# Gathering routed expert rows later in a group, and loading the next heads last: one change to an attention and mixture-of-experts kernel

## The chip, the cores and the metric

The kernel runs on one core of a Trainium2 chip. The metric is the device time of one execution in microseconds (us). The times shown are three runs, with their median, and one more execution that the hardware profiler took.

## The reference

The input x is (2, 2048, 256) in float32. What is computed is

```python
xn = layernorm(x)                                   # over the last axis
q, k, v = split(xn @ Wqkv); q, k = rope(q), rope(k) # 16 heads of 16
attn = softmax(causal(q @ k.T * scale)) @ v         # 2048 x 2048 scores per head
gates = softmax(xn @ gate_w.T + gate_b)             # 10 gates, 8 of them with an expert
w, sel = top_k(gates, 2); w = w on the 8 experts, scaled to sum to 1
ffn = sum over the two selected: w * (xn @ expert_w[sel] + expert_b[sel])
out = x + (attn @ Wout + bout) + ffn
```

## The kernel before, in words

Three stages follow each other: `project` (layer norm, q, k, v, gates, routing), `attend`, and `output` (the last projection and sums). The change lies in `attend`, which also carries the experts.

**Groups and units.** `attend` walks through 8 groups `g` of 4 heads (`GROUPS`). A group has `NU` = 40 units; unit `u` is one block of 128 keys against a chunk `c` of 512 queries. The chunks are walked in the order `WALK = (3, 2, 0, 1)`, so the units of chunk 3 are 0 to 15, of chunk 2 16 to 27, of chunk 0 28 to 31, of chunk 1 32 to 39; `ends` = (15, 27, 31, 39). Units that touch the causal diagonal (`diag[u]` is not None) are 1, 5, 8, 12, 17, 19, 22, 25, 28 to 31, 33, 34, 36 and 38.

**One unit on the engines.** TensorE (PE) computes 4 score matmuls (`scores`, line 1465), ScalarE (ACT) exponentiates each into `probs` (line 1216), GpSimd (POOL) zeroes the part above the diagonal if the unit is a diagonal one (`mask`, line 1110), and PE multiplies with the values, 4 matmuls, which the trace has as 8 (`pv`, line 1520; "PV u" below). `probs` has 4 buffers. PE waits in `pv` of a diagonal unit for `masked`, a count that `mask` raises. Between them PE computes scores for row maxima ("q" items, lines 1425 and 1428) that VectorE (DVE) reduces (line 1271), through two slots of `psP`. The order of PE's work in a group is written out by hand, a letter each (`PE_ORDER`): s a score matmul, p a PV, digits the q items, m a turned maximum, o a chunk's output, x and y the turn of an expert's input and the expert itself. The kinds of the groups are plain, route, four times experts, plain, last. "route" is "plain" with two more items r, the first ahead of PV 0 and the second behind PV 11; so group 6 has the same order as group 1 from PV 0 to PV 10.

**The experts.** In groups 2 to 5 each group runs 9 (`EG`) pairs of expert tiles. The result of a pair is copied by ACT from PSUM into `yt` (line 1237), and SP stores it to `expert_scratch` in HBM (`store_e`, line 1053, semaphore `y_stored`), then loads the weights of the pair after next (`load_e`, lines 1047 and 1049, semaphore `e_in`). `yt`, the weights and the inputs all lie in the space of `xn`.

**SP's queue.** SP issues its DMAs in the order of `PE_ORDER`. Behind the last unit of chunk 2 and of the last chunk (`FREED`), it waits for `pv_ok` of that unit and calls `load(g + 2, ...)`: 12 DMAs for `Qs`, 12 for `Ks`, one for `Vs` (line 74 and line 1030). In the experts order, the last PV (39) stands ahead of the last y (pair 8), so the loads are issued ahead of that pair's store. `store_m` (line 1041) stores the row maxima of a chunk.

**The gathers.** Each token takes two rows of `expert_scratch`, the first into `xn` (i = 0), the second into space of `Qs`, `Ks`, `Vs` and `rest` (i = 1): 32 tiles of 128 tokens each, so 64 indirect DMAs on POOL's queue (`gather`, line 1120). `fetched` says behind which unit a gather stands: in group 6 tile t with i = 0, in group 7 tile t with i = 1, each at `SPOTS[t]`, one gather behind a unit. `SPOTS` is 0 to 27 and 32 to 37. `passed` waits for the unit's last exponential. Since the first gather overwrites `xn`, POOL waits at the head of group 6 (lines 1159 to 1163) until every expert result is stored and every expert load has landed. POOL's instructions run in order, so that wait stands ahead of group 6's first mask, that of unit 1.

The first rows of all tiles are used in group 7 (`add_first`), the second in `output`.

Of the kernel before, what the change touches and what calls it, by code (L numbers as in the profile page):

```python
# [34 lines left out]
TT = N // P  # L35
TILES = B * TT
# [5 lines left out]
GROUPS = B * HEADS // HG  # L42
# [15 lines left out]
ONE = 1  # L58
# [726 lines left out]
def attend(nc, qk_s, v_s, we_s, be_s, xd, ys, wout, escale, idx, unscale, etab, Qs, Ks, Vs, xn, acc, hot, ge, eye, later, identf,  # L785
           identh, wo, on, wsel, bo, second, lane, number, at):
    with ExitStack() as ctx:
# [61 lines left out]
        pv_ok = sem("pv_ok")  # L849
# [15 lines left out]
        e_in = pair("e_in")  # L865
        hi_ok = sem("hi_ok")
        y_stored = pair("y_stored")
# [7 lines left out]
        WALK = (3, 2, 0, 1)  # L875
        FREED = {2: 1, 1: 0}
# [5 lines left out]
        units = [(c, kt) for c in WALK for kt in tiles(c)]  # L882
        NU = len(units)
        diag = [kt - CT * c if kt >= CT * c else None for c, kt in units]
        q0s = [0 if d is None else d * P for d in diag]
        ends = [u for u in range(NU) if u == NU - 1 or units[u + 1][0] != units[u][0]]
# [100 lines left out]
        def is_item(order, at):  # L987
            x = order[at]
            return x[0] in "moxyr" or x[0] == "q" and any(y[:-1] == x[:-1] for y in order[:at])
# [28 lines left out]
        def _(sp):  # L1018
# [51 lines left out]
            for g in range(GROUPS):  # L1070
                j, r = divmod(g, 2)
                order = orders[KIND[g]]
                n = 0
                for at, x in enumerate(order):
                    if x[0] == "m":
                        store_m(slot_of(n), uses(g, n), M_TURN[x[1:]], r ^ x[1], x[2])
                    elif x[0] == "y":

                        buf, _ = pair_of(g, x[1])
                        sp.wait_ge(item_ok[slot_of(n)], ONE + uses(g, n) + 1)  # L1080
                        sp.sem_inc(carrier, 1)
                        store_e(buf, EG * (g - 2) + x[1])
                        if EG * (g - 2) + x[1] + 2 < MTILES_USED // 2:
                            load_e(buf, EG * (g - 2) + x[1] + 2)
                    elif x[0] == "pv" and x[1] in ends and units[x[1]][0] in FREED and g < GROUPS - 2:

                        u = x[1]
                        sp.wait_ge(pv_ok, PV0 + NU * g + u + 1)
                        sp.sem_inc(carrier, 1)
                        load(g + 2, r, FREED[units[u][0]])  # L1090
                        if g == 1 and u == ends[1]:

                            sp.wait_ge(ids_ok, ONE + 1)
                            sp.wait_ge(bt_ok, ONE + 2)
                            for i in range(2):
                                load_e(i, i)
                    n += is_item(order, at)
            sp.wait_ge(wo_in, ONE + 16)

        @block.gpsimd  # L1100
        def _(pool):
# [17 lines left out]
            def gather(t, i):  # L1119
                nc.gpsimd.indirect_dma_start(out=xn[:, t, :] if i == 0 else second(t), out_offset=None, in_=ys[:, :],  # L1120
                                             in_offset=bass.IndirectOffsetOnAxis(ap=idx[:, i, t:t + 1], axis=0)
                                             ).then_inc(y_in[i], 16)
# [26 lines left out]
                    fetch(n + 2)  # L1149

            turned = {}
            fetched = {(6 + i, SPOTS[t]): (t, i) for i in range(2) for t in range(TILES)}

            for n in range(TILES):
                tables(n)
            for g in range(GROUPS):
                if g == 2:
                    split(0)
                if g == 6:

                    for i in range(2):
                        pool.wait_ge(y_stored[i], ONE + 16 * EG * 2)
                        pool.wait_ge(e_in[i], ONE + 16 * LOADS_E * EG * 2)
                if g == 7:

                    pool.wait_ge(pv_ok, PV0 + NU * g)
# [1 line left out]
                for at_x, x in enumerate([("s", 0, i) for i in range(SB)] + order):  # L1168
                    if x[0] == "s" and x[2] == HG - 1 and x[1] < NU:
# [15 lines left out]
                                fetch(n)  # L1185
                        if (g, u) in fetched:
                            passed(g, u)
                            gather(*fetched[g, u])
                    elif x[0] == "x":
                        n = EG * (g - 2) + x[1]  # L1190
                        turned[n] = slot_of(m), uses(g, m)
# [543 lines left out]
```

## Time and profile before

| | |
|---|---|
| median of 3 runs | 1041.32 us (1041.28 to 1044.14) |
| the profiled execution | 1037.85 us |
| its span | 1036.1 us |
| PE busy | 920.9 us, 89% of the span |
| DVE busy | 861.9 us, 83% |
| ACT busy | 714.8 us, 69% |
| POOL busy | 457.9 us, 44% |

A row of a timeline begins with the start and the duration in us, then the engine, the line, the operation, what is written and read, and how many instructions are merged ("x8"). In brackets stands how long the engine was idle just before, and what released it ("issue": nothing that the profile shows). "PEld" is PE loading weights. In a row of windows, each engine's busy time stands for the stretch with the number of instructions, then PE's granted clock as a share of 2.4 GHz, then what the DMA engines did.

### The profile page before, as it was taken

To read this page: it belongs to the slowest core of one execution; us is meant where nothing else is said; L and a number is where in the kernel's file an instruction comes from. 1 tells how busy PE (TensorE), PEld (TensorE's weight loads), DVE (VectorE), ACT (ScalarE), POOL (GpSimd) and SP (SyncE) were. 2 spreads that over 40 slices of the span, in tenths; PEclk is the share of its full clock that TensorE was granted. 3 is DMA by queue.
4 is the path that set the end of the run, shared out by engine and by line. 5 is a ranking of instruction groups with operands and counts; after the bars stand their busy time and mean duration, and the time that the engine had idled before them with its cause. 6 is when DMAs were issued, how large, how long until landed. Compare 5 with 4: busy or idle time off the path is not lost. (4 is left out here: it accounts for less than half of the span.)

```text
span 1036.1 us, 22141 instructions
## 1 busy us (share of the span) xinstructions
PE 920.9 (89%) x7874; PEld 388.0 (37%) x7874; DVE 861.9 (83%) x1132; ACT 714.8 (69%) x1542; POOL 457.9 (44%) x588
## 2 busy tenths in 40 slices
PE   3888435999999999999999999999999799999988
PEld 1554311333433234344333433344434323333257
DVE  6999779899899887987788787878798599995776
ACT  3556200788788777886787677877788588889942
POOL 4677559555201244244724564263423145345510
PEclk9999755899999999999999999999999899999999
DMA  9767530300200334054313443164505221112113
GB/s 323 265 240 267 168 127 5 110 2 28 76 2 2 114 104 134 3 172 135 123 43 112 134 133 95 53 164 130 128 12 150 78 65 59 32 47 63 47 51 123
DMA packets 82277, 106.65 MB, mean 103 GB/s; under 512 B 10192, under 2 KB 59256, under 8 KB 81144
## 3 DMA queue, kind: packets, MB, share of 16 engines
q1 hardware_dynamic: 75640, 87.40, 26.6%
q0 software_dynamic: 6528, 17.83, 6.5%
q8 instruction: 64, 1.05, 0.4%
q14 instruction: 45, 0.37, 0.1%
HBM read 67.37 MB, written 37.50 MB: 101 GB/s over the span
## 5 line engine op out<-in xcount | busy, mean ns | idle before, releaser
L1271 DVE TENSOR_REDUCE blk<-psP 128x2 f32<-128x1024 f32 (+2 forms) x576 | 640.2, 1161 | 102.8 <-PE psP L1428 43.5
L1216 ACT ACTIVATE probs<-psS 128x512 f32<-128x512 f32 (+3 forms) x1280 | 588.2, 539 | 189.9 <-PE psS L1465 170.5
L1465 PE MATMUL psS<-Qs,Ks 50*128 50x512 f16 (+3 forms) x1280 | 322.5, 354 | 12.4 <-ACT probs L1216 9.4
L1425 PE MATMUL psP<-Ks,Qs 48*128 48x512 f16 (+3 forms) x1280 | 284.7, 365 | 39.0 <-DVE blk L1271 21.9
L1520 PE MATMUL psO<-probs,Vs 128*32 128x512 f32 (+3 forms) x2560 | 301.4, 546 | 5.9 <-POOL probs L1110 4.9
L1110 POOL TENSOR_SCALAR_AFFINE_SELECT probs<-probs 128x512 f32<-128x512 f32 x128 | 82.4, 644 | 355.0 <-ACT probs L1216 338.5
L1465 PEld LDWEIGHTS psS<-Qs,Ks 50*128 50x128 f16 x1280 | 92.9, 94 | 239.1 <-ACT probs L1216 145.2
L1425 PEld LDWEIGHTS psP<-Ks,Qs 48*128 48x128 f16 x1280 | 75.5, 95 | 155.2 <-DVE blk L1271 100.8
L1428 PE MATMUL psP<-later,eye 64*128 64x128 bf16 x1024 | 91.0, 223 | 0.0
L1520 PEld LDWEIGHTS psO<-probs,Vs 128*32 128x32 f32 x2560 | 51.8, 108 | 87.1 <-issue 67.6
L1133 POOL DMA_INDIRECT xn<-norm_scratch,ids x72 | 69.5, 966 | 20.7 <-issue 11.5
L1428 PEld LDWEIGHTS psP<-later,eye 64*128 64x128 bf16 x1024 | 72.1, 99 | 16.9 <-issue 2.4
L1125 POOL TENSOR_SCALAR xn<-lane,at 128x128 f16<-128x128 f32 x64 | 38.6, 604 | 47.7 <-issue 24.1
L1497 PE MATMUL psP<-xn 128*128 128x256 f16 x432 | 57.3, 273 | 0.9 <-DVE xn L1306 0.9
L720 PE MATMUL psQ<-xp,wqp 128*128 128x512 f16 x192 | 47.6, 394 | 10.5 <-DVE turn L562 5.9
L1120 POOL DMA_INDIRECT xn<-expert_scratch,idx x32 | 30.4, 949 | 39.7 <-ACT probs L1216 20.9
L1497 PEld LDWEIGHTS psP<-xn 128*128 128x128 f16 x432 | 39.3, 98 | 21.4 <-DVE blk L1271 10.4
L1146 POOL TENSOR_TENSOR xn<-xn 128x512 f16<-128x512 f32 x36 | 41.8, 1161 | 3.0
L562 DVE TENSOR_TENSOR turn<-psQ,trig 128x1024 f32<-128x1024 f32 x32 | 38.4, 1218 | 2.6 <-DVE part L567 1.8
L1128 POOL TENSOR_SCALAR xn<-lane,at,number 128x76 f16<-128x76 f32 x64 | 39.5, 617 | 0.0
L1237 ACT COPY xn<-psP 128x512 f32<-128x512 f32 x36 | 21.1, 586 | 26.5 <-PE psP L1499 25.6
L364 POOL TENSOR_TENSOR turn<-turn 128x512 f32<-128x512 f32 x16 | 24.0, 1502 | 23.0 <-DVE turn L562 22.7
(171 smaller groups left out, 742.0 us busy)
## 6 DMA issues: line engine op xcount, KB each, us to landing
xn<-we_scratch SPq DMA_DIRECT2D x72, 256.0 KB
expert_scratch<-xn SPq DMA_DIRECT2D x36, 256.0 KB
v_scratch<-vst SPq DMA_DIRECT2D x8, 1024.0 KB, 4.0
qk_scratch<-part SPq DMA_DIRECT2D x32, 256.0 KB, 4.0
Vs<-v_scratch SPq DMA_DIRECT2D x16, 512.0 KB, 3.9
Ks<-qk_scratch SPq DMA_DIRECT2D x192, 32.0 KB
Qs<-qk_scratch SPq DMA_DIRECT2D x192, 32.0 KB
acc<-x SPq DMA_DIRECT2D x8, 512.0 KB, 9.1
```

The lines of the kernel that those rows point to most:

```text
L720: ins = pe.matmul(out, lhs(x, w, k), rhs(x, w, k), start=(n == 0), stop=(n == len(todo) - 1))
L1110: nc.gpsimd.affine_select(out=v, in_=v, compare_op=ALU.is_ge, fill=0.0, base=0, pattern=[[0, HG], [1, P]], channel_multiplier=-1).then_inc ...
L1128: nc.gpsimd.tensor_scalar(at_tile[:, n, :], lane[:, 0:MTILES], at[:, 0, n:n + 1], number[:, t:t + 1], ALU.is_equal, ALU.mult).then_inc(lis ...
L1133: nc.gpsimd.indirect_dma_start(out=xt[n % 2][:, t, :], out_offset=None, in_=xd[:, :], in_offset=bass.IndirectOffsetOnAxis(ap=ids[:, 2 * n ...
L1146: nc.gpsimd.tensor_tensor(xs[n % 2][:, 1, :], rows, xs[n % 2][:, 0, :], ALU.subtract).then_inc(x_split, 1)
L1216: nc.scalar.activation(probs[u % NPR][:, h, q0:CH], psS[:, n % SB, q0:CH], ACT.Exp, scale=exp_scale).then_inc(s_read[n % SB], 1)
L1271: nc.vector.tensor_reduce(out, src, AX.X, ALU.max).then_inc(item_ok[slot], 1)
L1425: ins = pe.matmul(psP[:, slot, at:at + w], Qs[r][rows, qt // CT, p, t * P:(t + 1) * P], Ks[r][rows, kc, p, 0:w], start=True, stop=True)
L1428: ins = pe.matmul(psP[:, slot, at + w - P:at + w], eye[all_rows, i, :], later[all_rows, i, :], start=False, stop=True, skip_group_check=True)
L1465: pe.matmul(psS[:, n % SB, q0:CH], Ks[r][rows, kt // CT, p, kt % CT * P:(kt % CT + 1) * P], Qs[r][rows, c, p, q0:CH], start=True, stop=Tru ...
L1497: pe.matmul(psP[:, slot, t * D:(t + 1) * D], xT[buf][:, w0, at_k:at_k + P], wt[2 * buf + t][:, of:of + D], start=(n == 0), stop=False)
L1520: ins = pe.matmul(psO[h * VW:(h + 1) * VW, q0:CH], Vs[r][:, kt, h * VW:(h + 1) * VW], probs[u % NPR][:, h, q0:CH], start=(kt == 0), stop=e ...
```

## The change

Two things are moved. On SP, the load for group g + 2 that follows the last unit of a group is issued at the very end of the group, behind all stores and expert loads. On POOL, the wait for the expert results moves from the head of group 6 to unit 6, and the 32 first-row gathers, which stood one behind each of 32 units from unit 0 on, stand two behind each of the 16 units 6 to 21. Group 7's gathers stay as they were.

```diff
-                    elif x[0] == "pv" and x[1] in ends and units[x[1]][0] in FREED and g < GROUPS - 2:
+                    elif x[0] == "pv" and x[1] in ends[:-1] and units[x[1]][0] in FREED and g < GROUPS - 2:
...
+                if g < GROUPS - 2:
+
+                    sp.wait_ge(pv_ok, PV0 + NU * g + NU)
+                    load(g + 2, r, FREED[WALK[-1]])
...
-            fetched = {(6 + i, SPOTS[t]): (t, i) for i in range(2) for t in range(TILES)}
+
+            fetched = {(6, SPOTS[6 + t]): [(2 * t, 0), (2 * t + 1, 0)] for t in range(TT)}
+            fetched.update({(7, SPOTS[t]): [(t, 1)] for t in range(TILES)})
...
-                if g == 6:
-
-                    for i in range(2):
-                        pool.wait_ge(y_stored[i], ONE + 16 * EG * 2)
-                        pool.wait_ge(e_in[i], ONE + 16 * LOADS_E * EG * 2)
...
                         if (g, u) in fetched:
                             passed(g, u)
-                            gather(*fetched[g, u])
+                            if (g, u) == (6, SPOTS[6]):
+
+                                for i in range(2):
+                                    pool.wait_ge(y_stored[i], ONE + 16 * EG * 2)
+                                    pool.wait_ge(e_in[i], ONE + 16 * LOADS_E * EG * 2)
+                            for t, i in fetched[g, u]:
+                                gather(t, i)
```

## Rows read from the trace of the kernel before

**Rows 1.** Waits of PE, 205 to 1010 us: total us, times, longest.
```profile
PE psO L1520 <- POOL probs L1110: 4.9, 3, 4.4
```
**Rows 2.** Timeline of PE where group 6 begins: PV 0 and PV 1.
```profile
815.71 1.06 PE L1520 MATMUL psO<-probs,Vs 128*32 128x512 f32 x8
...
825.60 1.93 PE L1520 MATMUL psO<-probs,Vs 128*32 128x512 f32 x8 [4.42 <-POOL probs L1110]
```
**Rows 3.** Timeline of POOL, same stretch: the first work of group 6.
```profile
823.91 0.98 POOL L1120 DMA_INDIRECT xn<-expert_scratch,idx  x1 [16.69 <-issue]
824.89 0.66 POOL L1110 TENSOR_SCALAR_AFFINE_SELECT probs<-probs 128x512 f32<-128x512 f32 x1
825.71 0.94 POOL L1120 DMA_INDIRECT xn<-expert_scratch,idx  x1 [0.16 <-issue]
826.96 0.95 POOL L1120 DMA_INDIRECT xn<-expert_scratch,idx  x1 [0.30 <-issue]
```
**Rows 4.** Timelines of ACT and SP, same stretch.
```profile
811.80 0.59 ACT L1237 COPY xn<-psP 128x512 f32<-128x512 f32 x1 [1.02 <-PE psP L1499]
...
810.25 4.07 SPq L74 DMA_DIRECT2D Qs<-qk_scratch  x12
...
818.97 0.51 SPq L1053 DMA_DIRECT2D expert_scratch<-xn  x1
```
**Rows 5.** Windows: PV 0 to 1, 1 to 3, 3 to 10, in groups 1 and 6.
```profile
278.31:283.71 5.40, 5.09 (x45) 2.15 (x45) 4.01 (x6) 3.91 (x9) 0.55 (x1) 1.00 0.42 124
283.71:288.66 4.95, 4.67 (x35) 1.11 (x34) 4.81 (x5) 4.16 (x10) 0.09 (x1) 1.00 0.19 55
288.66:304.28 15.62, 15.20 (x140) 4.52 (x140) 15.19 (x18) 13.30 (x30) 1.84 (x3) 1.00 0.01 2
815.71:825.60 9.89, 5.16 (x46) 2.14 (x45) 6.02 (x7) 5.94 (x12) 1.63 (x2) 0.79 0.40 116
825.60:832.83 7.23, 7.20 (x34) 1.42 (x34) 3.21 (x3) 3.10 (x8) 3.89 (x5) 0.58 0.31 90
832.83:848.45 15.62, 15.20 (x140) 4.51 (x140) 15.23 (x17) 13.27 (x30) 8.44 (x10) 1.00 0.21 60
```
**Rows 6.** Timeline of POOL in group 6: gathers of units 6, 7 and 24, mask of unit 25.
```profile
835.11 0.95 POOL L1120 DMA_INDIRECT xn<-expert_scratch,idx  x1 [0.65 <-ACT probs L1216]
837.57 0.95 POOL L1120 DMA_INDIRECT xn<-expert_scratch,idx  x1 [1.51 <-ACT probs L1216]
...
875.87 0.95 POOL L1120 DMA_INDIRECT xn<-expert_scratch,idx  x1 [1.37 <-ACT probs L1216]
876.99 0.64 POOL L1110 TENSOR_SCALAR_AFFINE_SELECT probs<-probs 128x512 f32<-128x512 f32 x1 [0.17 <-issue]
```
**Rows 7.** Timeline of PE in group 6: PV 17, 19 and 22.
```profile
862.37 1.06 PE L1520 MATMUL psO<-probs,Vs 128*32 128x512 f32 x8
867.63 0.85 PE L1520 MATMUL psO<-probs,Vs 128*32 128x384 f32 x8
874.68 0.64 PE L1520 MATMUL psO<-probs,Vs 128*32 128x256 f32 x8
```
**Rows 8.** Timeline of DVE around PV 17 to 22 of group 6.
```profile
867.50 8.61 DVE L1271 TENSOR_REDUCE blk<-psP 128x2 f32<-128x768 f32 x8 [0.47 <-PE psP L1428]
```
**Rows 9.** Timeline of SP and PE, end of group 4 into group 5: first load, last weight load, third expert.
```profile
701.56 4.09 SPq L74 DMA_DIRECT2D Qs<-qk_scratch  x12
...
703.52 0.59 ACT L1237 COPY xn<-psP 128x512 f32<-128x512 f32 x1 [1.43 <-PE psP L1499]
...
720.70 0.29 SPq L1049 DMA_DIRECT2D xn<-be_scratch  x1
...
733.39 0.83 PE L1497 MATMUL psP<-xn 128*128 128x256 f16 x6
```
**Rows 10.** Window of one microsecond behind group 7's last PV.
```profile
995.00:996.00 1.00, 0.53 (x3) 0.56 (x4) 0.63 (x2) 0.00 (x0) 0.00 (x0) 0.75 0.00 0
```
**Rows 11.** Timeline of POOL, the longest gather, in group 7.
```profile
984.08 1.24 POOL L1120 DMA_INDIRECT rest<-expert_scratch,idx  x1 [0.34 <-ACT probs L1216]
```

## The prediction

> **What bounds the kernel now.** I read the page's shares first: PE is busy for 89% of the span and DVE for 83%, so within `attend` a stall of PE costs time unless DVE had work left. Then the waits of PE over the whole of `attend`: it hardly ever waits for a mask, 4.9 us in 3 waits, and 4.4 us of that is one wait [rows 1]. The timeline places it at PV 1 of group 6: PE had nothing to run for 4.42 us, and then ran PV 1 in 1.93 us instead of 1.06 us [rows 2], with the clock at its lower level (the granted share over PV 0 to 1 is 0.79, over PV 1 to 3 it is 0.58, where 1.00 is 2.4 GHz [rows 5]). The timeline of POOL says why. Its first work in group 6 is the first gather at 823.91, after 16.69 us of idleness, and only behind it comes the mask of unit 1, at 824.89 [rows 3]. POOL stood in the wait for the last expert result. ACT had copied that result by 812.39, but SP was then busy with the 25 loads that began at 810.25, and issued the store at 818.97 [rows 4]; 4.94 us later POOL went on.
>
> What the stall costs in all can be measured, since group 1 has the same order of work from PV 0 to PV 10 and no gather or wait on POOL. From PV 0 to PV 3 group 1 takes 5.40 + 4.95 = 10.35 us, group 6 takes 9.89 + 7.23 = 17.12 us. From PV 3 to PV 10 both take 15.62 us, though POOL is busy for 8.44 us of it in one and 1.84 us in the other [rows 5]. So the stall with its slow clock costs **6.77 us** (4.49 before PV 1, 2.28 behind it), nothing of it is won back later, and single gathers behind a unit cost PE nothing.
>
> **Part 1: the loads behind the store.** Nothing is added or removed, 25 DMAs change places with the last pair's store and, in groups 2 to 4, with its 4 weight loads. In group 5 the store can be issued at about 812.4 instead of 818.97, 6.6 us earlier; with the same 4.94 us behind it, POOL would go on at 817.4, and the mask of unit 1 would be done at 817.4 + 0.98 + 0.66 = 819.0, before PE comes to PV 1 at 825.60 - 4.42 = 821.18. This part alone would thus remove the stall. What is moved behind it: the loads start when ACT's copy is done, about 2.5 us later (in group 4, 701.56 to 704.11 [rows 9]). The heads that they bring are first read in the middle of the next group, some 40 us on, and the row maxima whose store is queued behind them are first read at chunk 0, later still; both are covered. The tightest follower is the third expert of the next group. Its weights are issued by 720.99 and its matmuls start at 733.39 [rows 9]. 2.5 us later leaves 9.9 us for the landing. The trace doesn't show that landing; the store that POOL waited for took 4.94 us including its wake-up, and the page's transfers of the same 256 KB have medians of 2.1 to 7.8 us. All of these fit, so I cost it at nothing, with 0 to 3 us (1 us in each of three groups) as bounds.
>
> **Part 2a: the wait moved from the head to unit 6.** The mask of unit 1 no longer has a wait or a gather ahead of it. Unit 6's last exponential is done at 835.11 in the old times [rows 6], so 828.3 with the stall gone; the store landed at about 817.4. The moved wait therefore finds its count reached, with some 11 us to spare. Either part removes the stall, together they do no more than one of them: **-6.77 us**, bounded by -4.42 (only the idle time goes and the clock still falls) and -6.77.
>
> **Part 2b: two gathers behind a unit.** The number of gathers in group 6 stays 32. But they now fill 16 units, and POOL needs for each unit two steps of 1.25 us (825.71 to 826.96 [rows 3]), so 2.50 us, while a unit lasts about 2.23 us (PV 3 to 10, 15.62 us in 7 units [rows 5]). With masks between them POOL falls behind, and the masks stand in its queue behind the gathers. I worked this out in the old times, without the shift of 6.77 that is common to all. POOL starts the first pair at 835.11, ends it at 837.61, and unit 7 is ready at 837.57 [rows 6], so from there on POOL never waits for ACT. A gather step that leads to a mask takes 0.98 us [rows 3] to 1.12 us [rows 6], I take 1.05; a mask start to the next gather takes 0.82 us (824.89 to 825.71 [rows 3]); and a mask that ends at 825.55 releases PV at 825.60.
> - Mask 17: 22 gathers, 3 of them ahead of a mask, and 2 masks: 19 x 1.25 + 3 x 1.05 + 2 x 0.82 = 28.5, so it starts at 863.65 and lets PV 17 start at 864.3. PE wants it at 862.37 [rows 7]: 2.0 us late.
> - Mask 19: 26 gathers, 34.2 us, PV 19 at 870.0 instead of 867.63 [rows 7]: 2.3 us late.
> - Mask 22: 32 gathers, 27 x 1.25 + 5 x 1.05 + 4 x 0.82 = 42.3, PV 22 at 878.1 instead of 874.68 [rows 7]: **3.4 us late**.
>
> Masks 8 and 12 are in time by the same count. The three don't add up, because a PE that has been held back arrives later at the next mask; what stays is the last and largest. Of it DVE saves a little: it had reductions left, and worked from 867.50 to 876.11 without a gap [rows 8], so a short stall of PE is partly filled. How much of its lead it gets back in each of three places is not to be seen; between 0 and 1.4 us, and I take 0.4, as DVE's only gaps there are of 0.47 us [rows 8]. That makes **+3.0 us**. The bounds: if the second gather of a pair needed only the 0.16 us gap that follows a mask [rows 3] instead of 0.30, a step would be 1.11, 16 such steps save 2.2 us, and with 1.0 from DVE the price is about 0.2; with no help from DVE and 0.03 us more per step it is 4.2. I take 3.0, because the step of 1.25 is what several gathers in a row took. Units 22 to 39, which lose their gathers, gain nothing, since those cost nothing.
>
> **Sum.** -6.8 + 3.0 = -3.8 us. The profiled execution would go from 1037.85 to 1034.1. The median of the runs lies 3.5 us above it, and I carry the difference over: 1041.32 - 3.8 = **1037.5 us**. The measurement can tell about 0.3% (3.1 us) from no change, and the forecast lies just beyond that.
>
> [...] The longest gather in the trace, in group 7, takes 1.24 us [rows 11], the others 0.95. [...]
>
> **Rivals.**
> 1. *The pairs are free.* If a pair is quick enough, or DVE's lead covers the late masks, all of the 6.8 us is kept: 1034.5. For it: PV 3 to 10 took the same with and without gathers [rows 5]. Against it: those were single, and 2.50 us is more than a unit's 2.23.
> 2. *The new stalls lower the clock.* Behind the last PV, a microsecond in which PE was busy for 0.53 us already has a share of 0.75 [rows 10]. If a stall of 2 us at PV 17 does the same, slow matmuls add about as much as behind the old stall, 2.28 us, less what POOL catches up meanwhile: some 2.1 us net, so 1039.6, no measurable change. Against it: DVE rather than PE sets the pace there. The Trainium skill ("TensorE: Matmul & The Clock Gate", section "What's actually happening") also has idleness lead to the lower level; it would say this rival is possible, not how likely.
> 3. *Slower: POOL's queue of indirect DMAs fills up.* 32 gathers with hardly a pause were never run before. If a step takes not 1.25 but 1.54 us (the 1.24 us gather [rows 11] plus 0.30), mask 22 is late by another 9 us, and the kernel ends 5.5 us later than before: 1046.8. It decides from 1.37 us a step, where 3.8 us more eat the forecast gain.
> 4. *The change doesn't reach the stall*, because the store lands after unit 6, or PV 1 waits for something else: 1041. The 11 us to spare speak against it.
> 5. *Late weights* in groups 3 to 5 take back up to 3 us: about 1040.
>
> **Chances.** The forecast 0.57, rival 1 0.13, rival 2 0.17, rival 3 0.06, rivals 4 and 5 together 0.07. Of the forecast's 0.57, the price of the pairs lies below 3.7 us in about three of four cases, which is faster by over 0.3%: 0.43. With rival 1 that is 0.56 faster; rival 3 gives 0.05 slower; the remaining 0.39 is within 0.3%. The range goes from 1034.0 (rival 1) to 1041.3 (rivals 2, 4 and 5), and leaves out rival 3 and some scatter of the runs.
>
> **What would show it.** Right: no wait of PE for POOL at PV 1 of group 6, the clock at 1.00 there, PV 0 to PV 3 in about 10.4 us; SP's store of the last pair directly behind ACT's copy; gathers of group 6 at 1.25 us one after the other from unit 6, and PE waiting for POOL at PV 17 (about 2 us), PV 19 and PV 22. Wrong: no wait of PE for a mask (rival 1), a share below 1.00 around PV 17 (rival 2), steps of 1.4 us and more (rival 3), a new wait of POOL at unit 6 (rival 4), or the third expert's matmuls waiting (rival 5).

## The result: slower by 1%, and the profile after

| | before | after |
|---|---|---|
| median of 5 runs | 1042.81 us (1041.28 to 1044.14) | 1052.51 us (1049.71 to 1054.24) |
| the profiled execution | 1037.85 us | 1050.31 us |
| its span | 1036.1 us | 1048.5 us |
| PE busy | 920.9 us | 932.5 us |
| DVE, ACT, POOL busy | 861.9, 714.8, 457.9 us | 862.6, 715.1, 458.0 us |

The ratio of after to before is **1.0101** (95% interval 1.0075 to 1.0126). The forecast was 1037.5 us, and a gain.

The engines' totals on the page of the kernel after are nearly those of before. Only PE is busy for 11.6 us more, though it runs the same number of matmuls. The granted clock (section 2 of the page, a digit for each fortieth of the span) is below full speed in one slice behind 80% of the span; the kernel before has such a slice just ahead of it.

```profile
PEclk9999755999999999999999999999999989999999
```

**The old stall is gone, exactly as forecast.** The timeline of PE in the kernel after has PV 0, 1, 2 and 3 of group 6 with no wait. PV 0 to PV 3 takes 828.04 - 817.70 = 10.34 us, and the clock is at 1.00 throughout (the second block, columns as in [rows 5]), where [rows 2, 5] had the stall and a lower share.

```profile
817.70 1.06 PE L1527 MATMUL psO<-probs,Vs 128*32 128x512 f32 x8
823.09 1.07 PE L1527 MATMUL psO<-probs,Vs 128*32 128x512 f32 x8
...
828.04 1.06 PE L1527 MATMUL psO<-probs,Vs 128*32 128x512 f32 x8
```

```profile
817.70:828.04 10.34, 9.75 (x78) 3.26 (x78) 9.29 (x10) 9.00 (x19) 0.73 (x2) 1.00 0.39 111
```

Timelines of ACT and SP in the same execution: the store of the last pair is issued 0.09 us behind the copy that ends at 814.38, ahead of all 25 loads, where [rows 4] had it behind them.

```profile
813.79 0.59 ACT L1244 COPY xn<-psP 128x512 f32<-128x512 f32 x1 [1.02 <-PE psP L1506]
...
814.47 0.38 SPq L1053 DMA_DIRECT2D expert_scratch<-xn  x1
814.90 4.14 SPq L74 DMA_DIRECT2D Qs<-qk_scratch  x12
```

The timeline of POOL in group 6 of the kernel after. The first gather waits for unit 6's exponential and not for the store. The steps are 1.28, 1.26 and 1.25 us, and a mask follows a gather at once: all as counted from [rows 3, 6]. But then POOL waits for ACT, twice for over 2.5 us, where the sum had POOL late and PE waiting for it.

```profile
830.33 0.98 POOL L1124 DMA_INDIRECT xn<-expert_scratch,idx  x1 [1.75 <-ACT probs L1223]
831.61 0.95 POOL L1124 DMA_INDIRECT xn<-expert_scratch,idx  x1 [0.30 <-issue]
832.87 0.94 POOL L1124 DMA_INDIRECT xn<-expert_scratch,idx  x1 [0.31 <-ACT probs L1223]
834.12 0.95 POOL L1124 DMA_INDIRECT xn<-expert_scratch,idx  x1 [0.30 <-issue]
...
843.32 0.95 POOL L1124 DMA_INDIRECT xn<-expert_scratch,idx  x1 [2.55 <-ACT probs L1223]
...
860.24 0.95 POOL L1124 DMA_INDIRECT xn<-expert_scratch,idx  x1 [2.62 <-ACT probs L1223]
```

**Where the time is.** ACT's copies of a chunk's result (the lines `ot<-psO`) end the chunks, so their distance is the time of a chunk. I read it the same way in every trace; nearly every comparison below uses it.

| us from one chunk end to the next | before | after | the sum made of it |
|---|---|---|---|
| group 6, chunk 3 (units 0 to 15) | 48.95 | 54.43 | 42.2 |
| group 6, chunk 2 (units 16 to 27) | 26.69 | 31.75 | 29.7 |
| group 6, chunks 0 and 1 | 7.32, 15.11 | 7.31, 15.11 | unchanged |
| group 7, all four chunks | 84.76 | 84.78 | unchanged |

(48.95 less 6.77; 26.69 plus 3.0.) Group 6 begins at 810.20 before and at 812.19 after, 2.0 us later; of that 1.5 us arise in the first chunk of group 2, where these executions spread by as much from chip to chip and run to run (below), so I count it as scatter. Chunks 3 and 2 of group 6 hold the rest: 86.18 - 75.64 = **+10.5 us**, where 71.9 us was forecast.

**What they wait for.** A timeline of all engines of the kernel after, from 836 us. The score matmuls (`psS`, `psP`) are done, yet ACT and DVE, idle meanwhile, begin on them only 1.0 to 1.5 us later. For these late starts the profile mostly names "remote" as the releaser: a signal came in that it can put down to no engine and no DMA queue.

```profile
836.03 0.60 PE L1432 MATMUL psP<-Ks,Qs 48*128 48x512 f16 x2
837.14 0.95 POOL L1124 DMA_INDIRECT xn<-expert_scratch,idx  x1 [0.30 <-issue]
837.67 1.23 DVE L1278 TENSOR_REDUCE blk<-psP 128x2 f32<-128x1024 f32 x1 [1.78 <-remote]
...
840.64 0.38 PE L1432 MATMUL psP<-Ks,Qs 48*128 48x512 f16 x1
841.97 3.04 ACT L1223 ACTIVATE probs<-psS 128x512 f32<-128x512 f32 x6 [1.61 <-PE psS L1472]
842.04 3.49 DVE L1278 TENSOR_REDUCE blk<-psP 128x2 f32<-128x1024 f32 x3 [1.72 <-remote]
...
855.08 0.48 PE L1435 MATMUL psP<-later,eye 64*128 64x128 bf16 x4
857.04 1.23 DVE L1278 TENSOR_REDUCE blk<-psP 128x2 f32<-128x1024 f32 x1 [2.61 <-remote]
857.76 1.09 ACT L1223 ACTIVATE probs<-psS 128x512 f32<-128x512 f32 x2 [2.19 <-remote]
858.32 0.61 PE L1432 MATMUL psP<-Ks,Qs 48*128 48x512 f16 x2 [2.09 <-issue]
```

The matmul of 840.64 ends at 841.02 and DVE begins at 842.04; those of 855.08 end at 855.56 and DVE begins at 857.04. Of the waits of the kernel after for 812 to 900 us (total us, times, longest) these are four rows, and "remote" has the first and the third: up to 3.5 us of idle time at once. The kernel before has no "remote" wait in group 6.

```profile
DVE blk L1278 <- remote: 10.8, 6, 3.5
DVE blk L1278 <- PE psP L1435: 6.2, 7, 1.6
ACT probs L1223 <- remote: 3.9, 2, 2.2
ACT probs L1223 <- PE psS L1472: 21.4, 26, 2.0
```

The windows of the kernel after from 838 us (columns as in [rows 5]) have PE's clock at 0.83, 0.98 and 0.68. Worked out from the share, 0.83 means that a third of the 10 us ran at the 1.2 GHz level and delayed PE by at most 1.7 us, and 0.68 by at most 3.2 us. The three come to 5.1 us, and 6.8 us with the window of 878 to 888 us, which has 0.83 again. So the late starts and the slow matmuls that follow them share the loss.

```profile
838.00:848.00 10.00, 7.40 (x48) 1.66 (x45) 7.05 (x7) 5.26 (x12) 5.75 (x7) 0.83 0.28 80
848.00:858.00 10.00, 7.00 (x78) 3.44 (x78) 5.27 (x9) 5.24 (x11) 6.36 (x8) 0.98 0.30 84
858.00:868.00 10.00, 9.68 (x55) 2.02 (x55) 7.26 (x7) 6.83 (x14) 4.63 (x6) 0.68 0.22 66
```

Windows of one microsecond in the same trace show which comes first. From 841 to 842 us PE, DVE, ACT and POOL are all idle while the clock is still at 1.00 (DVE and ACT start late, PE and POOL wait for ACT); at 0.50, the lower level, it is only from 844 us on:

```profile
841.00:842.00 1.00, 0.02 (x1) 0.00 (x0) 0.00 (x0) 0.03 (x1) 0.00 (x0) 1.00 0.45 123
844.00:845.00 1.00, 1.00 (x8) 0.11 (x8) 1.00 (x2) 1.00 (x3) 0.69 (x2) 0.50 0.07 16
```

### The profile page after: what moved, and what is told of

It is laid out like the page before. It is cut to its first block and busy times, and to the rows that moved or that the text cites. A ratio compares the mean times of both kernels' runs of the same rounds, so it can differ in the third digit from the quotient of the medians.

```text
span 1048.5 us, 22135 instructions
## 1 busy us (share of the span) xinstructions
PE 932.5 (89%) x7874; PEld 390.5 (37%) x7874; DVE 862.6 (82%) x1132; ACT 715.1 (68%) x1542; POOL 458.0 (44%) x588
## 5 line engine op out<-in xcount | busy, mean ns | idle before, releaser
L1472 PE MATMUL psS<-Qs,Ks 50*128 50x512 f16 (+3 forms) x1280 | 326.1, 356 | 15.9 <-ACT probs L1223 10.4
L1432 PE MATMUL psP<-Ks,Qs 48*128 48x512 f16 (+3 forms) x1280 | 287.6, 368 | 39.8 <-DVE blk L1278 22.0
L1527 PE MATMUL psO<-probs,Vs 128*32 128x512 f32 (+3 forms) x2560 | 305.9, 552 | 1.0 <-ACT ot L1216 0.5
```

The costliest lines, as they stand in the source:

```text
L1432: ins = pe.matmul(psP[:, slot, at:at + w], Qs[r][rows, qt // CT, p, t * P:(t + 1) * P], Ks[r][rows, kc, p, 0:w], start=True, stop=True)
L1472: pe.matmul(psS[:, n % SB, q0:CH], Ks[r][rows, kt // CT, p, kt % CT * P:(kt % CT + 1) * P], Qs[r][rows, c, p, q0:CH], start=True, stop=Tru ...
L1527: ins = pe.matmul(psO[h * VW:(h + 1) * VW, q0:CH], Vs[r][:, kt, h * VW:(h + 1) * VW], probs[u % NPR][:, h, q0:CH], start=(kt == 0), stop=e ...
```

## The experiments

The theories, in words (the expectations use their own short names, which are not these letters; they also weigh that the loss depends on the chip, and that it takes both parts of the change together): (a) POOL's own time: two gathers behind a unit make the masks late, as in the forecast; (b) the gathers themselves, issued in a row, hold up something that ACT and DVE wait for; (c) it is not the gathers but their neighbours: POOL being busy without a pause, or bytes moving on the DMA engines; (d) the moved loads of part 1 do it. The kernels ran on five chips, each known by a number; each is compared with the kernel before on its own chip. The kernel before alone has medians of 1029.1 (chip 12), 1027.6 (11), 1028.2 (7), 1040.7 (6) and 1038.4 us (13), and 1042.8 us on the occasion of the result, so there are **two kinds of occasion**, a quick and a slow one, and the sets on chips 12, 11 and 7 must be read with that in mind. Each chip was used once, so nothing here tells whether the kind belongs to the chip or to the time; "kind of chip" below stands for either.

### On chip 12: one part alone, and one gather behind a unit

`p1_loads_last` is the kernel before with the change to SP's queue alone:

```diff
-                    elif x[0] == "pv" and x[1] in ends and units[x[1]][0] in FREED and g < GROUPS - 2:
+                    elif x[0] == "pv" and x[1] in ends[:-1] and units[x[1]][0] in FREED and g < GROUPS - 2:
...
+                if g < GROUPS - 2:
+
+                    sp.wait_ge(pv_ok, PV0 + NU * g + NU)
+                    load(g + 2, r, FREED[WALK[-1]])
```

> Part 1 alone: only SP's order is changed, POOL's wait stays at the head of group 6 and its gathers stay single. Theory A (gathers in close succession hold up the other engines): -6.8 us against the kernel before, PV 0 to PV 3 of group 6 in about 10.4 us. Theory B (masks queued late on POOL are the whole loss): the same -6.8 us. Theory C (the moved loads are what costs, by colliding with later transfers): slower than before, or no gain. A and B are told apart by the other kernels of this call.

`p2_pairs_only` is the changed kernel with these lines put back as before, so it has the change to POOL's queue alone:

```diff
-                    elif x[0] == "pv" and x[1] in ends[:-1] and units[x[1]][0] in FREED and g < GROUPS - 2:
+                    elif x[0] == "pv" and x[1] in ends and units[x[1]][0] in FREED and g < GROUPS - 2:
...
-                if g < GROUPS - 2:
-
-                    sp.wait_ge(pv_ok, PV0 + NU * g + NU)
-                    load(g + 2, r, FREED[WALK[-1]])
```

> Part 2 alone: the wait at unit 6 and two gathers behind each of units 6 to 21, SP's order as before. Theory A and theory B: the whole loss of the full change is here, so +8 to +11 us against the kernel before. Theory C: -4 us, as the prediction had it for part 2 (stall gone, masks 3 us late).

`singles_from_2` has both parts, but one gather behind each of units 2 to 27 and 32 to 37:

```diff
-            fetched = {(6, SPOTS[6 + t]): [(2 * t, 0), (2 * t + 1, 0)] for t in range(TT)}
+            fetched = {(6, SPOTS[2 + t]): [(t, 0)] for t in range(TILES)}
...
-                            if (g, u) == (6, SPOTS[6]):
+                            if (g, u) == (6, SPOTS[2]):
```

> The full change, but one gather behind each of the 32 spots from unit 2 on (2 to 27, 32 to 37), and the wait at unit 2. Theories A and B: the stall at PV 1 is gone and nothing is lost, -6.8 us against the kernel before. Theory C: slower than before or no gain. If the wait at unit 2 comes too early for the store, POOL idles there and a mask is late: less gain, to be seen as POOL idle at unit 2.

`singles_and_filler` adds to it, behind units 6 to 21, two operations on POOL (0.62 and 0.32 us in its trace). A unit's work takes POOL 2.0 us with them (829.96 to 831.99), where a pair of gathers takes 2.5:

```diff
...
+                            if g == 6 and 6 <= u < 22:
+                                pool.wait_ge(filled, ONE + 2 * (u - 6))
+                                nc.gpsimd.tensor_tensor(c9_f, bo[:, :], bo[:, :], ALU.add).then_inc(filled, 1)
+                                nc.gpsimd.memset(gq_b[:, :, :], 0.0).then_inc(filled, 1)
```

> As the kernel with single gathers from unit 2, and behind each gather of units 6 to 21 POOL also runs an addition over 128x256 and a memset over 128x256 that nobody reads, some 1.3 us in all, as long as a second gather. POOL is as full as with pairs, but has no second gather. Theory A: the gain of the single gathers is kept up to the 3 us or so of late masks that the prediction worked out, so -3.5 to -6.8 us. Theory B: as much slower as the pairs, +8 us or more, with PE waiting for POOL.

| chip 12 | median us | ratio to before | group 6, chunk 3 / 2 |
|---|---|---|---|
| before | 1029.05 | | |
| p1_loads_last | 1020.94 | 0.9938 [0.9916, 0.9959] | 42.18 / 26.68 |
| p2_pairs_only | 1023.33 | 0.9957 [0.9936, 0.9978] | 41.90 / 29.94 |
| singles_from_2 | 1022.03 | 0.9948 [0.9929, 0.9968] | 42.18 / 26.68 |
| singles_and_filler | 1022.72 | 0.9945 [0.9926, 0.9965] | 45.73 / 26.69 |

Either part alone takes the stall away, as forecast. The two theories that expected 8 us or more of loss in `p2_pairs_only` missed: it is faster than before by 0.4%. With the loads moved alone the kernel is faster by 0.6%, which speaks against theory (d), though on a chip where nothing is slower than before; the chips 6 and 13 settle it, since all kernels with single gathers there have the moved loads too. And on this chip theory (a) holds. POOL and PE in the timeline of `p2_pairs_only`: the gathers follow each other in steps of 1.25 us up to 844.90, mask 17 can begin only behind them, and PV 17 waits 1.95 us for it; mask 19 begins at 851.37 and mask 22 at 859.38, and PE has no wait for either.

```profile
843.65 0.95 POOL L1120 DMA_INDIRECT xn<-expert_scratch,idx  x1 [0.30 <-issue]
844.90 0.95 POOL L1120 DMA_INDIRECT xn<-expert_scratch,idx  x1 [0.30 <-issue]
845.86 0.64 POOL L1110 TENSOR_SCALAR_AFFINE_SELECT probs<-probs 128x512 f32<-128x512 f32 x1
...
846.56 1.06 PE L1523 MATMUL psO<-probs,Vs 128*32 128x512 f32 x8 [1.95 <-POOL probs L1110]
850.17 1.71 PE L1523 MATMUL psO<-probs,Vs 128*32 128x512 f32 x8
```

PV 18, at 850.17, takes 1.71 us instead of 1.06: rival 2 shows in small, with a share of 0.81 and 0.85 around the stall. Against the single gathers the pairs cost 71.84 - 68.86 = **2.98 us**, where 3.0 was forecast. Counted from PV 0 in both kernels, PV 17 comes 1.73 us later than with single gathers, PV 19 2.99 us, and PV 22 2.98 us (PV 0 begins at 810.34 here and at 810.57 in `singles_from_2`, PV 22 at 860.12 and 857.37). So the wait gives 1.7 us and the slow matmuls behind it the other 1.3; the masks 19 and 22 add nothing.

```profile
845.00:850.00 5.00, 3.44 (x37) 1.92 (x37) 2.68 (x7) 1.83 (x4) 4.22 (x5) 0.81 0.37 100
850.00:855.00 5.00, 4.75 (x44) 1.79 (x45) 3.39 (x5) 3.38 (x7) 3.92 (x6) 0.85 0.31 89
```

So nothing here explains a slower kernel. `singles_and_filler` lost 3.6 us in chunk 3 in its profiled execution, where the clock fell to 0.50 for 5 us with no late mask; that did not return in two later executions of the same kernel (42.78 and 42.85 us), and I have no cause for it.

### On chip 11: the whole change again

`full_change` is the changed kernel, unedited; `before_traced` is the kernel before, unedited, for its trace on this chip. The other two are shown against `singles_from_2`: `pairs_every_second` puts the pairs behind units 2, 4, ... 26 and 32, 34, 36, and `fours_every_fourth` four gathers behind units 2, 6, ... 26 and 34:

```diff
-            fetched = {(6, SPOTS[2 + t]): [(t, 0)] for t in range(TILES)}
+            fetched = {(6, SPOTS[2 + 2 * t]): [(2 * t, 0), (2 * t + 1, 0)] for t in range(TT)}
...
-            fetched = {(6, SPOTS[2 + t]): [(t, 0)] for t in range(TILES)}
+            fetched = {(6, SPOTS[2 + 4 * t]): [(4 * t + k, 0) for k in range(4)] for t in range(8)}
```

> The changed kernel itself, beside the same runs of the kernel before as the others of this call. Its first trace lost 10.5 us in group 6 (chunk 3 took 54.4 us, chunk 2 31.8 us), where part 2 alone lost only 3.0 us against single gathers. Theory D (what is lost depends on the chip: the same code holds up the handoffs between engines on one chip and not on another): where the kernel before has about 50.0 us in chunk 3 of groups 3 to 5, the full change is as fast as part 2 alone, -3.8 us against the kernel before. Theory E (the two parts together do what neither does alone, the moved loads meeting the pairs): about +10 us on any chip.

> The kernel before, unchanged, for a trace on the same chip. Theory D: its groups 2 to 5 show on this chip either no wait of DVE and ACT with a remote release (then chunk 3 takes about 50.0 us), or such waits as in the first trace (50.7 to 52.5 us), and the full change follows it. Theory E says nothing of it. The stall at PV 1 of group 6 is there on any chip, 4.4 us.

> The full change with two gathers behind every second of the 32 spots, from unit 2 on (16 pairs), and the wait at unit 2. POOL has no more to do than with single gathers. Theory F (it is the adjacency of two gathers that costs): slower than single gathers from unit 2 by several us. Theory B' (it is POOL's fill, more than a unit's time for each unit, that makes masks late): as fast as the single gathers, -6.8 us against the kernel before, within 1 us.

> Four gathers behind every fourth spot from unit 2 on (8 times four, behind units 2, 6, 10, 14, 18, 22, 26 and 34). Four take 5.0 us of POOL at once. Theory B': only a mask that falls due in those 5 us is late; masks follow the fours at units 12, 19, 22 and 25 with 2.2 us or more of slack, so at most 1 us is lost against the single gathers. Theory F: each four holds the others up for 1 us or more, in all 8 us or more lost, no gain against the kernel before.

| chip 11 | median us | ratio to before | group 6, chunk 3 / 2 |
|---|---|---|---|
| before (before_traced) | 1027.61 (one run: 1025.76) | | 48.96 / 26.69 |
| full_change | 1026.58 | 0.9989 [0.9971, 1.0006] | 41.92 / 29.95 |
| pairs_every_second | 1022.27 | 0.9947 [0.9927, 0.9966] | 42.18 / 26.71 |
| fours_every_fourth | 1021.17 | 0.9938 [0.9913, 0.9963] | 42.21 / 26.78 |

The same kernel that took 86.18 us for the two chunks takes 71.87 us here, which is the forecast's sum of 71.9. Its windows have a clock of 1.00 up to 845 us, just ahead of PV 17 at 846.74, and it has no "remote" wait at all, nor has `before_traced`; what DVE waits for in 800 to 880 us is PE, and one mask is 2.0 us late:

```profile
825.00:835.00 10.00, 9.55 (x103) 3.75 (x103) 9.35 (x14) 8.44 (x19) 7.76 (x9) 1.00 0.38 107
835.00:845.00 10.00, 9.65 (x79) 2.72 (x76) 9.91 (x9) 9.21 (x19) 7.58 (x8) 1.00 0.35 105
845.00:855.00 10.00, 8.12 (x78) 3.69 (x78) 6.07 (x11) 5.21 (x12) 8.05 (x10) 0.83 0.33 94
```

```profile
DVE blk L1278 <- PE psP L1435: 5.8, 6, 1.9
PE psO L1527 <- POOL probs L1114: 2.0, 1, 2.0
```

The 12 runs of this kernel spread from 1023.41 (the profiled one) to 1031.39 us, and so do the 25 of before, from 1022.97 to 1031.77. The profile thus shows the best of them, and its 3.2 us to the median are not explained by it. Pairs with a pause between them, and even fours, cost nothing here.

### On chip 7: the neighbours of the gathers

`full_change_2`, `singles_from_2_b` and `filler_b` are `full_change`, `singles_from_2` and `singles_and_filler` again. `singles_and_sp_loads` adds bytes instead of POOL's work: SP loads 128 KB behind each of units 6 to 21, into space that is free.

```diff
...
+                    elif x[0] == "pv" and g == 6 and 6 <= x[1] < 22:
+                        k = x[1] - 6
+                        sp.wait_ge(pv_ok, PV0 + NU * g + x[1] + 1)
+                        if k >= 2:
+                            sp.wait_ge(extra[k % 2], 16 * (k // 2))
+                        sp.dma_start(spare if k % 2 else c9_f, xd[k * P:(k + 1) * P, :]).then_inc(extra[k % 2], 16)
...
```

> The changed kernel once more, since what it lost differed by 10 us between two occasions. Theory D (the loss depends on the chip or its state, not on the code alone): it follows the kernel before of this call. If that one is near 1027 us, the full change is within 0.5% of it and its trace has no remote release before DVE and ACT; if that one is near 1042 us, it is about 1% slower and the trace has them in group 6. Theory E (the parts together): slower by 10 us wherever it runs; the first repetition speaks against it.

> Single gathers from unit 2, on the same chip as the full change. Theory D with late handoffs behind gathers in a row: on a chip that has them, the gap to the full change is 13 us or more; on a chip without, 3 to 4.5 us, of which 3.0 are the late masks of units 17 to 22.

> Single gathers and POOL arithmetic in the place of the second ones, which had lost 3.6 us in chunk 3 of group 6 in its first trace with no mask late, from a dip of the clock. On a chip with late handoffs: as the single gathers if it is the descriptors of the gathers that hold the others up, as the pairs if it is POOL being busy. On a chip without: -5 to -7 us against the kernel before, and the dip may be there or not.

> Single gathers from unit 2, and SP loads 128 KB from HBM behind each PV of units 6 to 21 of group 6, as many bytes as a second gather moves, into tiles that nobody reads. POOL has no more to do. If the bytes on the DMA engines hold the others up: as slow as pairs on that chip. If it is POOL's own work on a gather: as fast as the single gathers, within 1 us.

| chip 7 | median us | ratio to before | group 6, chunk 3 / 2 |
|---|---|---|---|
| before | 1028.21 | | |
| full_change_2 | 1023.92 | 0.9961 [0.9936, 0.9985] | 41.91 / 29.94 |
| singles_from_2_b | 1022.25 | 0.9934 [0.9911, 0.9957] | 42.18 / 26.68 |
| filler_b | 1021.80 | 0.9929 [0.9900, 0.9957] | 42.78 / 26.69 |
| singles_and_sp_loads | 1021.94 | 0.9937 [0.9912, 0.9963] | 42.18 / 26.69 |

A third chip without the loss. Here the whole change is a gain of 0.4%, as part 2 alone was on chip 12, and its profile is the forecast's. Since there is no loss, this set can't tell the theories apart; it says that the filler costs 0.6 us at most and the loads nothing where the pairs cost their 3 us.

### On chip 6: the loss comes back

The same four kernels under new labels.

> The changed kernel on a fourth chip. Theory D: near 1024 us with the kernel before near 1028 us, and 3.0 us of late masks in group 6; or, on a chip or in a state with late handoffs, near 1052 us with the kernel before near 1042 us and remote releases in group 6. Theory E (the two parts together): about 10 us slower than before on this chip too.

> Single gathers from unit 2 on the same chip: 3 us faster than the full change without late handoffs, 13 us or more with them.

> POOL arithmetic in the place of the second gathers: within 1 us of the single gathers without late handoffs. With them: as the single gathers if a gather's descriptors are the cause, as the full change if POOL being busy is.

> SP loads of the same bytes in the place of the second gathers: within 1 us of the single gathers without late handoffs. With them: as the full change if the bytes on the DMA engines are the cause, as the single gathers if not.

| chip 6 | median us | ratio to before | group 6, chunk 3 / 2 |
|---|---|---|---|
| before | 1040.65 | | |
| full_change_3 | 1048.01 | **1.0066** [1.0039, 1.0093] | **54.34 / 31.31** |
| singles_from_2_c | 1033.27 | 0.9924 [0.9905, 0.9943] | 42.18 / 26.69 |
| filler_c | 1033.30 | 0.9927 [0.9913, 0.9941] | 42.85 / 26.68 |
| sp_loads_c | 1033.34 | 0.9942 [0.9915, 0.9968] | 42.18 / 26.69 |

This set decides. Here the changed kernel is slower than before again, by nearly the two chunk times of the result, and its waits for 800 to 880 us again hold "remote":

```profile
DVE blk L1278 <- remote: 9.8, 5, 2.7
ACT probs L1223 <- remote: 5.6, 2, 2.9
```

As in the result, all engines are idle at once: from 836 to 837 us of its trace PE, DVE, ACT and POOL are busy for 0.00 us.

`singles_from_2_c`, on the same chip and with the same 32 gathers one by one, has no such wait in group 6 and is 14.7 us faster. The filler keeps POOL busy for 9.24 of 10 us in a window of its trace (`filler_c`), with the clock at 1.00, more than the pairs do in any window shown here, and costs next to nothing: POOL's being busy is not the cause.

```profile
835.00:845.00 10.00, 8.84 (x99) 3.38 (x91) 9.35 (x12) 7.70 (x18) 9.24 (x16) 1.00 0.21 61
```

Nor are bytes: 128 KB behind each of 16 units, loaded by SP beside the single gathers, leave the chunks as they are. Theory (c) falls in both forms, and (d) with it, since all three kernels have the moved loads. Theory (b) stays: what differs is that indirect DMAs follow each other on POOL with nothing between them. One control is missing: the pairs without the moved loads (`p2_pairs_only`) were not run on this kind of chip, so that the two parts are needed together isn't excluded. The last of the moved loads is issued by 823.57 in the trace of the result, though, and the first pair at 830.33.

### On chip 13: a cure tried elsewhere, and pairs with pauses

If rows of indirect DMAs are the cause, they should act wherever they stand. In groups 2 to 5 `fetch` (line 1137) issues the input rows of an expert pair with two indirect DMAs, one behind the other. `fetches_apart` is `singles_from_2` with the second of them moved behind the next unit's last exponential, or ahead of the next turned input if that comes first (the diff is against `singles_from_2`):

```diff
-            def fetch(n):
-                for t in range(2):
+            pending = []
+
+            def fetch(n, ts=(0, 1)):
+                for t in ts:
...
-                    fetch(n + 2)
+                    fetch(n + 2, (0,))
+                    pending.append(n + 2)
...
+                        if pending:
+                            passed(g, u)
+                            fetch(pending.pop(), (1,))
...
+                        if pending:
+                            fetch(pending.pop(), (1,))
```

`pairs_every_second_b` is `pairs_every_second` again, for this kind of chip.

> Single gathers from unit 2, and in groups 2 to 5 the second fetch of a pair (line 1133) is issued behind the next unit's last exponential instead of right behind the first. If fetches in a row cost the groups 2 to 5 their 1 to 2 us each where handoffs are late: 3 us or more faster than the single gathers there, so -10 us against the kernel before. On a chip without late handoffs: as the single gathers, -5 to -7 us, or up to 1 us less where a fetch comes too late.

> Isolated pairs of gathers behind every second unit. With late handoffs on this chip: as the single gathers (-7 us) if only an unbroken row of gathers holds the others up, 3 us or more slower than that if a pair is enough. Without: -5 to -7 us as before.

| chip 13 | median us | ratio to before | group 6, chunk 3 / 2 |
|---|---|---|---|
| before | 1038.42 | | |
| fetches_apart | **1020.40** | **0.9824** [0.9790, 0.9858] | 42.19 / 26.69 |
| pairs_every_second_b | 1032.74 | 0.9946 [0.9928, 0.9964] | 42.40 / 27.27 |

POOL's timeline of the kernel after (first) and of `fetches_apart` (second): between the two fetches there were 0.31 us, and now there are 2.80.

```profile
395.23 0.98 POOL L1137 DMA_INDIRECT xn<-norm_scratch,ids  x1 [0.27 <-POOL xn L1150]
396.51 0.95 POOL L1137 DMA_INDIRECT xn<-norm_scratch,ids  x1 [0.31 <-issue]
```

```profile
392.58 0.98 POOL L1139 DMA_INDIRECT xn<-norm_scratch,ids  x1 [0.27 <-POOL xn L1152]
396.36 0.95 POOL L1139 DMA_INDIRECT xn<-norm_scratch,ids  x1 [2.80 <-ACT probs L1231]
```

`fetches_apart` has no "remote" wait anywhere in its trace. `pairs_every_second_b`, whose fetches are in pairs, has these in the whole of its trace:

```profile
ACT probs L1223 <- remote: 5.9, 4, 1.8
DVE blk L1278 <- remote: 1.8, 1, 1.8
```

One of ACT's four stands at 897.60, in group 6 beside the pairs with pauses; the others lie in groups 2 to 4.

| chunk 3, us, in group | 2 | 3 | 4 | 5 |
|---|---|---|---|---|
| before (result's occasion) | 50.73 | 52.13 | 52.52 | 50.70 |
| pairs_every_second_b, chip 13 | 50.16 | 51.59 | 51.48 | 50.51 |
| fetches_apart, chip 13 | 49.35 | 50.49 | 50.43 | 50.07 |
| full_change, chip 11 | 49.43 | 49.98 | 49.97 | 50.01 |

The two medians lie 12.3 us apart, the spans of the two traces 15.7 us, since the profiled execution of `pairs_every_second_b` is its longest. In the traces groups 2 to 5 hold 9.9 us of this, and that is where the fetches were changed. The first four fetches, in a row in group 1, stand in both kernels as they were, and the chunk that they fall into, chunk 2, takes 27.5 us in both, where it takes 26.7 on the quick chips; no "remote" wait marks this, so the word shows only part of the loss. Group 6 holds 2.2 us: 42.40 + 27.27 - 42.19 - 26.69 = 0.8 us in chunks 3 and 2, and 1.4 us in chunks 0 and 1. So pairs with a pause cost little on this kind of chip, but not nothing. Group 7 and what follows hold the other 3.8 us, where the two kernels are the same, so not all of the difference is the edit's. `singles_from_2` itself, the control that differs by the fetches alone, was run on chip 6 (0.9924 of before) and not on this one. `fetches_apart` has the lowest ratio to before of all: it beats the kernel before by 18.0 us, and by more the changed one, which took 1.0101 and 1.0066 of before on this kind. How it does on the other kind of chip, where `full_change` already had short chunks, was not run.

## Why the prediction was wrong, point by point

- **The stall and its price (parts 1 and 2a): right.** PV 0 to PV 3 in 10.34 us (10.4 was forecast). Group 6's two chunks go from 75.64 to 68.87 us with single gathers: -6.77 us, as the sum had it. The moved wait is never the last one.
- **Late weights (rival 5): nothing.** The first chunks of groups 2 to 5 take 49.4 to 50.0 us in `full_change`, and 49.5 to 50.0 us in `before_traced` on the same chip, whose loads are not moved. Rivals 1 and 4 did not occur either: pairs in a row were free on no chip, and POOL found its count reached at unit 6.
- **POOL's count for the pairs (part 2b): right where nothing else acts.** Steps of 1.25 us, PV 17 waiting 1.95 us (2.0), the net price 2.98 us (3.0), on three chips of five. There the two chunks take 71.9 us, and the change makes no measurable difference on chip 11 and is a gain of 0.4% on chip 7, as is part 2 alone on chip 12. That the price came out so exactly is in part luck, for it is made up otherwise: the sum had waits at PV 17, 19 and 22 and no slow clock (3.4 less 0.4), and measured were one wait and 1.3 us of slow matmuls behind it, which is rival 2. That did not come on top, because mask 22 ends at 860.03 and would have held PV 22 until then in any case; it began at 860.12.
- **The failed step** is the bound of that price: "between 0.2 and 4.2 us", worked out from POOL's time alone. I let the pairs cost only what they take on their own engine, because single gathers cost nothing [rows 5]. On the occasion of the result the term is 86.18 - 68.87 = **17.3 us instead of 3.0** (68.87 is what single gathers take on the chips 12, 7 and 6, and 68.88 on 13), by a way that the sum didn't have: beside an unbroken row of indirect DMAs ACT and DVE start late and stand idle for up to 3.5 us at a time, PE and POOL then wait for ACT, and the clock falls to 0.83 and 0.68 behind it. That the row is the condition is shown by chip 6 (pairs 85.65 us; the same gathers single 68.87, with filler 69.53, with loads 68.87) and by chip 13 (pairs with a pause 69.67). A pause between the pairs also halves the number of gathers in a stretch, so whether the missing pause or the rate counts is not told apart. What holds ACT and DVE up is only named "remote" by the profile; it is not shown.
- **Rival 3 had the side and the place, and the wrong mechanism.** It had POOL's own queue fill and the step grow from 1.25 to 1.54 us. The step stayed at 1.25, and PE had no wait for a mask in group 6. Its 1046.8 us was closer to the result than the forecast, with a chance of 0.06.
- **The sign that was there.** The waits of the kernel before, over the whole trace, have "remote" for both engines:

```profile
DVE blk L1271 <- remote: 8.9, 4, 2.5
ACT probs L1216 <- remote: 5.7, 3, 1.9
```

  All of them stand in groups 1 to 4 beside the fetches, of which two follow each other, and at 335 to 340 us four. On the quick chips no trace has one. One of them, in the timeline of DVE:

```profile
470.67 1.23 DVE L1271 TENSOR_REDUCE blk<-psP 128x4 f32<-128x1024 f32 x1 [2.44 <-remote]
```

  I read only the groups beside the change and the gathers of group 6, which stood singly, and had no price for two in a row. Groups 1 to 5 fetch 36 times two in a row; at 8.9 us for 36, the 16 pairs of group 6 would have added 4.0 us (an estimate), and turned the forecast's -3.8 into no gain. Even that was too little for a row without a pause.

**What stays open.** What it is that holds ACT and DVE up; why three chips show none of this and three occasions do, and whether that belongs to the chip or to the time; whether the occasion of the result was one of the chips 6 and 13; how long a row must be and how long the pause. On chip 11 the runs of both kernels spread by 8 to 9 us, and a trace shows only one of them.

## What to carry to other kernels

Spread indirect DMAs on POOL one by one between other work, also where they look free on their own engine: with nothing between them they can delay engines that never wait for them. Before a count of instructions on one engine is taken for the price of a change, look in the waits for a releaser that is no engine ("remote"), and at what stands beside it. And compare with the kernel before on the same chip and occasion: 9 to 15 us lay between the two kinds for one kernel, as much as the whole change was worth on either.

## What the runs showed of the hardware that I had not expected

- The kernel before takes 1027.6 to 1029.1 us on three chips and 1038.4 to 1042.8 us on the others. On chip 13 the fetches apart, with single gathers and the moved loads, took 18.0 us off, some 11 us more than the old stall's 6.8, together with every "remote" wait.
- A gather's own duration (0.95 us) and step (1.25 us) did not change while DVE waited 10.8 us and ACT 3.9 us for "remote" beside it. In two traces PE, DVE, ACT and POOL were idle together for about 1 us (841 to 842 us of the result's, 836 to 837 us of `full_change_3`'s), though finished matmuls lay ready for DVE.
- On chip 6, chunk 1 of group 7 took 18.2 us in `full_change_3` and 18.8 to 19.2 us in the three other kernels there, instead of the 13.9 of most traces. The timeline of `full_change_3` shows two masks in 7.77 us beside a long row of DVE's sums, and PE waiting for them; the three others show the same 7.8 us:

```profile
985.87 13.51 DVE L1378 SCALAR_TENSOR_TENSOR acc<-xn,wsel,acc 128x256 f32<-128x256 f32 x32
992.69 7.77 POOL L1114 TENSOR_SCALAR_AFFINE_SELECT probs<-probs 128x512 f32<-128x512 f32 x2
999.92 1.08 PE L1527 MATMUL psO<-probs,Vs 128*32 128x256 f32 x8 [4.26 <-POOL probs L1114]
```

  In the trace of the result these two masks take 0.86 and 0.93 us beside the same row of DVE's, and 0.64 us is a mask's usual time. The Trainium skill ("SBUF — State Buffer", section "SBUF: two separate sides") says that a VectorE operation with two SBUF inputs and a GpSimd operation that reads SBUF exclude each other at a shared port pair. The masks and these sums are such operations, and the 7.77 us fit it; but the same rows stood beside each other on the chips 7, 11 and 12 and in the result without that loss, so the rule alone does not tell when it comes.
- In group 6 no DVE operation with two SBUF inputs stands beside the delayed starts: DVE reduces PSUM there (the rows from 836 us on). So that rule does not describe what the change lost.
